# Two transformer-like layers on one core: who makes the sign tiles of the attention, where a head's sum stands, and where held sums and activation tables are prepared

## The reference, cut to what matters

```python
q, k, v = heads(x @ Wq + bq), heads(x @ Wk + bk), heads(x @ Wv + bv)      # 16 heads of 16
proj = gelu(x4.reshape(B, T, H * D) @ W1 + b1) @ W2 + b2                  # one score a token and head, of q and of k
q_proj, k_proj = (each centred, over one common deviation)
Z = concatenate([k_proj, q_proj]); idx = argsort(Z)
vc = v - mean(v over tokens)
# sorted by Z, with running sums: for each query the sum over all keys with a smaller score
context = z_q * cumsum(vc) - cumsum(vc * z)
norm = 2 * (z_q * cumsum(1) - cumsum(z)) - (z_q * total_v - total_vz)
context = 2 * context / max(norm, 1e-4)
```

## Time and profile before

| | us |
|---|---|
| median of 3 runs (lowest to highest) | 1379.29 (1377.48 to 1381.62) |
| the profiled execution | 1386.35 |
| its span | 1385.0 |
| PE busy, share of the span | 1080.4, 78% |
| DVE busy | 960.1, 69% |
| ACT busy | 818.6, 59% |
| POOL busy | 354.9, 26% |

### The profile page before, as it was taken

The page is one execution under the profiler, slowest core; times in us unless marked ns, Lnnn a source line. Parts: engine busy times, 40 slices in busy tenths (PEclk is TensorE's granted clock), DMA queues, the critical chain, the costliest instruction groups (busy, mean ns, idle before and its releaser), DMA issues. The chain is left out here.

```text
span 1385.0 us, 30980 instructions
## 1 busy us (share of the span) xinstructions
PE 1080.4 (78%) x12566; PEld 932.0 (67%) x12566; DVE 960.1 (69%) x1709; ACT 818.6 (59%) x957; POOL 354.9 (26%) x381
## 2 busy tenths in 40 slices
PE   5365689798898899979998897665548948983797
PEld 3254686598888887658888886554348845652797
DVE  5111686889999995889999996255626647843465
ACT  7111454699999954489999996143413326660332
POOL 3745001100000000200004401571644421345344
PEclk9689699899999999979999999795669979966799
DMA  8953400311212100012123213554243450013343
GB/s 252 340 149 122 157 1 0 74 63 63 93 63 94 63 2 0 4 62 94 63 74 113 90 67 101 199 199 145 89 135 104 120 179 1 1 47 108 112 119 100
DMA packets 83824, 133.72 MB, mean 97 GB/s; under 512 B 14083, under 2 KB 70403, under 8 KB 79043
## 3 DMA queue, kind: packets, MB, share of 16 engines
q1 hardware_dynamic: 65440, 91.27, 20.9%
q0 software_dynamic: 12960, 35.60, 7.1%
q10 hardware_dynamic: 5286, 4.88, 1.1%
HBM read 84.18 MB, written 47.54 MB: 95 GB/s over the span
## 5 line engine op out<-in xcount | busy, mean ns | idle before, releaser
L1655 ACT ACTIVATE b_signs<-b_q_everywhere,normed 128x2048 bf16<-128x2048 f32 x224 | 429.9, 1993 | 13.4 <-PE banks L1537 13.0
L1537 PE MATMUL banks<-b_value_parts,b_signs 128*128 128x102 bf16 x8192 | 398.3, 209 | 46.1 <-DVE b_signs L1872 39.6
L1537 PEld LDWEIGHTS banks<-b_value_parts,b_signs 128*128 128x128 bf16 x8192 | 377.9, 98 | 64.4 <-DVE b_signs L1872 49.1
L1872 DVE TENSOR_SCALAR b_signs<-b_q_everywhere,normed 128x2048 bf16<-128x2048 f32 x288 | 352.7, 1279 | 4.7 <-PE banks L1537 4.6
L850 POOL DMA_INDIRECT moe_slots<-normed,slot_of_token x128 | 135.7, 1060 | 39.1 <-issue 35.2
L1924 POOL MEMSET b_value_parts<- 128x256 bf16 x2 | 2.6, 1310 | 404.6 <-PE banks L1385 404.6
L415 PE MATMUL banks<-identity 128*128 128x128 f32 x264 | 45.7, 351 | 53.7 <-issue 24.3
L379 DVE BATCH_NORM_STATS2 ln_stats<-residual 128x6 f32<-128x256 f32 x192 | 71.4, 417 | 17.1 <-SPq L2147 9.7
L415 PEld LDWEIGHTS banks<-identity 128*128 128x128 f32 x264 | 44.2, 264 | 54.5 <-issue 33.5
L406 ACT ACTIVATE normed<-residual,ln_shift,ln_rstd 128x256 f32<-128x256 f32 x128 | 67.9, 592 | 11.9 <-DVE ln_shift L401 11.8
L487 PE MATMUL banks<-identity,normed 128*128 128x128 f32 x256 | 51.8, 338 | 25.5 <-ACT normed L406 21.1
(11 more groups left out here) (292 smaller groups left out, 2299.3 us busy)
## 6 DMA issues: line engine op xcount, KB each, us to landing
b_q_everywhere<-q_rows SPq DMA_DIRECT2D x32, 1024.0 KB
normed<-expert_rows SPq DMA_DIRECT2D x6, 1024.0 KB, 10.0
d_rows<-moe_slots SPq DMA_DIRECT2D x39, 129.5 KB
f_rows<-moe_slots SPq DMA_DIRECT2D x39, 129.5 KB
moe_slots<-a_empty SPq DMA_DIRECT2D x8, 518.0 KB, 10.3
a_rows<-moe_slots SPq DMA_DIRECT2D x16, 259.0 KB
c_rows<-moe_slots SPq DMA_DIRECT2D x16, 259.0 KB
expert_rows<-a_empty SPq DMA_DIRECT2D x1, 4096.0 KB
```

Of the source, the lines that this page charges most:

```text
L1537: ins = nc.tensor.matmul(banks[qt // QPB][:, qt % QPB * VP:(qt % QPB + 1) * VP], t.SG[:, (hh * TB + kt) % RING, qt * P:(qt + 1) * P], t.VO ...
L1655: nc.scalar.activation(t.SG[:, g % RING, :], t.QB[:, hh % 2, :], ACT.Sigmoid, bias=t.NKT[:, kt, hh % H:hh % H + 1], scale=STEEP).then_inc( ...
L1872: nc.vector.tensor_scalar(t.SG[:, g % RING, :], t.QB[:, hh % 2, :], t.KTM[:, kt, hh % H:hh % H + 1], 1.0, ALU.is_gt, ALU.mult).then_inc(s. ...
```

## The change

The diff, shortened where a line is only the new spelling of a count:

```diff
-WARM_SENT, WARM_ROWS, WARM_HEADS, WARM_PAIR = 16, 12, 28, 4
+WARM_SENT, WARM_ROWS, WARM_HEADS, WARM_PAIR, WARM_PARTS = 28, 16, 28, 4, 8
...
-DVE_KT = tuple(t for t in range(TB) if t not in ACT_KT)
+EVEN_HEADS = (6, 12, H - 1)
...
+def act_tiles(h):
+    return ACT_KT + (TB - 1,) if h in EVEN_HEADS else ACT_KT
+
+def dve_tiles(h):
+    return tuple(t for t in range(TB) if t not in act_tiles(h))
...
@@ pe_parts
             nc.tensor.matmul(value_bank(k, n - 1)[:, :], k.MINUSI[:, :], value_columns(t, n - 1, False, 1), start=False,
                              stop=True).then_inc(s.a_left, 1)
+        if n == 2:
+            pe_held(k, batch)
+        if n in (4, 6, 8):
+            if n == 4:
+                nc.tensor.wait_ge(s.held, batch + 1)
+            pe_warm(k, k.bank[4], WARM_PARTS)
@@ pe_held
-    nc.tensor.wait_ge(s.nkt, batch + 1)
     nc.tensor.wait_ge(s.qtm, batch + 1)
+    nc.tensor.wait_ge(s.ones_set, batch + 1)
+    nc.tensor.wait_ge(s.kz_third, batch + 1)
@@ pe_head
-        nc.tensor.wait_ge(s.ones_set, batch + 1)
-        nc.tensor.wait_ge(s.kz_third, batch + 1)
-        pe_held(k, batch)
     if hh >= 2:
         nc.tensor.wait_ge(s.sum, hh - 1)
-    if h == 1:
-        nc.tensor.wait_ge(s.held, batch + 1)
...
@@ act_attention
-            for kt in ACT_KT:
+            for kt in act_tiles(h):
                 act_sign(k, batch * H + h, kt)
@@ act_prepare
     if batch:
         act_norms_early(k)
+    nc.scalar.activation(t.ZS[:, 1:2], k.EPS[0:H, 0:1], ACT.Gelu)
     for n in range(steps + 1):
...
     for p in range(2, 4):
         act_part(k, batch, p, 0)
+    nc.scalar.activation(t.ZS[:, 1:2], k.EPS[0:H, 0:1], ACT.Sigmoid)
     for n in range(PAIRS + 1):
@@ dve_attention
-            for kt in DVE_KT:
+            for kt in dve_tiles(h):
                 dve_sign(k, hh, kt)
-                if h == 0 and kt == 6:
-                    dve_held(k, batch)
-                if h and kt == 2:
+                if h and kt == 4:
                     dve_sum(k, hh - 1)
                 for group in made:
-                    if kt in CONTEXT_KT:
+                    if kt in CONTEXT_KT and (h, kt) != (H - 1, CONTEXT_KT[-1]):
                         dve_context(k, batch, group, CONTEXT_KT.index(kt))
...
+        dve_context(k, batch, len(TOGETHER) - 2, len(CONTEXT_KT) - 1)
         dve_sum(k, batch * H + H - 1)
@@ dve_prepare, the loop over pairs
             dve_rest_of_values(k, batch, n + 1)
+        if n == 4:
+            dve_held(k, batch)
         if n == 2:
```

More of the change, by code:

```diff
@@ L132, in group_of, with act_made, dve_made @@
     return next(i for i, (lo, hi) in enumerate(TOGETHER) if lo <= h < hi)
+def act_tiles(h):
+    return ACT_KT + (TB - 1,) if h in EVEN_HEADS else ACT_KT
+def dve_tiles(h):
+    return tuple(t for t in range(TB) if t not in act_tiles(h))
+def act_made(hh):
+    return sum(len(act_tiles(i % H)) for i in range(hh))
+def dve_made(hh):
+    return TB * hh - act_made(hh)
 def cut_of(t):
@@ L1293, in sp_attention @@
             if h >= 2:
-                nc.sync.wait_ge(s.sign_d, len(DVE_KT) * (hh - 1))
-                nc.sync.wait_ge(s.sign_a, len(ACT_KT) * (hh - 1))
+                nc.sync.wait_ge(s.sign_d, dve_made(hh - 1))
+                nc.sync.wait_ge(s.sign_a, act_made(hh - 1))
             nc.sync.dma_start(t.QB[:, hh % 2, :], k.zq_rows[hh, :].partition_broadcast(P)).then_inc((s.qb_in0, s.qb_in1)[hh % 2], 16)
@@ L1531, in pe_head @@
                                  t.HELD3[:, h, :].unsqueeze(1).broadcast_to([P, QPB, 6]), start=False, stop=False)
-        if kt in ACT_KT:
-            nc.tensor.wait_ge(s.sign_a, len(ACT_KT) * hh + ACT_KT.index(kt) + 1)
+        if kt in act_tiles(h):
+            nc.tensor.wait_ge(s.sign_a, act_made(hh) + act_tiles(h).index(kt) + 1)
         else:
-            nc.tensor.wait_ge(s.sign_d, len(DVE_KT) * hh + DVE_KT.index(kt) + 1)
+            nc.tensor.wait_ge(s.sign_d, dve_made(hh) + dve_tiles(h).index(kt) + 1)
         for qt in range(TB):
@@ L1729, in dve_prepare @@
             if i == 0 and batch:
-                nc.vector.wait_ge(s.sign_a, len(ACT_KT) * H * batch)
+                nc.vector.wait_ge(s.sign_a, act_made(H * batch))
             z = t.Z[:, q, ch * BANK:(ch + 1) * BANK]
@@ L1865, in dve_sign @@
     g = hh * TB + kt
-    if kt == DVE_KT[0]:
+    if kt == 0:
         nc.vector.wait_ge((s.qb_in0, s.qb_in1)[hh % 2], 16 * (hh // 2 + 1))
```

## The result

The changed kernel takes 1373.32 us (median of 6 runs, 1368.7 to 1374.93); six runs of the kernel before, beside it, have a median of 1379.99. The ratio is 0.9957, with a 95% interval of 0.9942 to 0.9972: 0.43% faster, some 5.9 us by the ratio, where 9.8 were forecast. The profiled execution took 1373.54 (span 1372.3, mean granted clock 0.914). It is 12.8 us under that of before, more than the medians differ, because the stages outside the attention also came out shorter in it. These repeat within 0.1 to 0.4 us in the kernels that have the same code there, on three chips.

What follows compares the result with a forecast made beforehand. DVE was taken to bound the heads, ACT 3% behind, with ACT the bound in heads 0 to 2. Heads -8.5, start -2.7, GELU +1.45 gave -9.8 us: 1369.5, its own range 1366 to 1373, overall 1363.5 to 1376.5.

Steps and rivals of the forecast that it cites:

- The heads: Attention heads: moved sum and handed-over signs gain 2.2 us (batch 0), 3.9 (batch 1), 1.2 per last head; 8.5 in all.
- Rival A: Heads 3 to 14: ACT takes over as the bound, leaving a gain of 5.0 us, 1374.3; chance 0.22.
- The groups of head 6 and 12 keep 41.7: Sign that ACT bounds: three-head groups with a handed-over sign still take 41.7 us.
- The start of the heads: Each batch's first heads: early table load and moved held sums bring ACT's first sign 1.35 us earlier, 2.7 in all.
- take half of 2.95 at full clock: Value parts: PE's 16 held matmuls, moved there, take half of 2.95 us and end at 263.8.
- Rival D: Value parts: the clock falls despite the unread matmuls, 2.2 us less gain, 1371.7; chance 0.60 shared with the main forecast.
- The GELU: First rows of each batch: the unread GELU and its table load cost 1.45 us in batch 0, nothing in batch 1.
- The drain: ACT's table switches: the skill page adds a 1.38 us drain to each; by it the kernel would be 1.4 us faster.
- The runs of unread matmuls: Ahead of the expert stages: the longer warm-up runs lie hidden in PE's waits and change nothing, 0 us.
- rival B: Four expert stages: longer warm-up runs keep the clock up for the first rows, 6 us in all, 1363.5; chance 0.12.
- the sign set for B: Sign that the longer runs help: the stages before 190 and behind 845 change their length.
- Rival C: Heads: PE runs dry behind the third sign and its clock falls, +10.7 us each; one per batch 1390.9; chance 0.04.

Runs made afterwards that it cites:

- e3: The kernel before with only the edits of the head loops: 1372.76 us, ratio 0.9952.
- e5: The changed kernel with no signs handed over to ACT, the sum still behind the third sign: 1352.01 us, ratio 0.9972 to before on its chip.
- e6: The changed kernel with the sum behind the second sign again, signs still handed over: 1354.47 us, ratio 0.9984 to before on its chip.
- e12: e8 with one more sign handed to ACT, in head 9 of batch 1: 1364.32 us, ratio 0.9878 to the kernel before.
- e9: The changed kernel with the 16 held matmuls reading a contiguous block of ones, held values left wrong: 1367.82 us, ratio 0.9919 to before.
- e2: The changed kernel with the held values' matmuls and small steps back at head 0: 1369.01 us, ratio 0.9915 to the kernel before.
- e11: e8 with the 16 held matmuls shared between two accumulator banks, half of each held sum left out: 1365.37 us, a single run.
- e8: The changed kernel without the unread GELU and with the held values back at head 0: 1343.83 us, ratio 0.9903 to before on its chip.
- e1: The changed kernel without the unread GELU: 1370.49 us, ratio 0.9925 to the kernel before.
- e7: The changed kernel with the warm-up runs ahead of the expert stages short again (16 and 12 matmuls): 1349.54 us, ratio 0.9942 to before on its chip.
- e4: The changed kernel without the head-loop edits, except the moved last context step of group 4: 1379.41 us, ratio 1.0002 to the kernel before.

## Why the prediction was right, and where it was wrong

**The heads: right.** Forecast 2.2, 3.9 and 2 x 1.2, together 8.5; measured 1.97, 4.13, and 1.68 and 0.70 for the two last heads: 8.5. e3 shows the same 8.5 with nothing else changed. The reason held too: DVE bounds, the sum behind the third sign finds PE's tile done (0.1 of idle in e5), and the lost signs then count (e6 shows that they don't without it). Between DVE's sums a group of three heads takes 41.67 to 41.70 before; in the change it takes 40.60 where a sign is handed over and 41.79 where none is. The difference is the one sign of 1.20; the 0.12 more in every group comes with the sum's new place (e5 has 41.79 to 41.80 in all four), and it is why 1.97 came and not 2.4.

That the two last heads came to the forecast 2.4 is in part luck. Between DVE's sums head 15 takes 13.21 instead of 15.30 in both batches, 2.09 less. PE's start of head 15 cuts this into 1.68 and 0.70, as PE is 0.60 ahead of DVE's sum there in batch 0 and 1.59 ahead in batch 1 (0.20 in both before).

One reading was wrong. The prediction took ACT's 165.5 in batch 1 for a sum of overlapping durations, about 161 with two more signs. It is the time in which ACT was busy, the window less its idle time, and with the two signs it became 167.86 of 169.71: ACT was nearly as close to the bound as DVE. It did not spoil the 3.9.

**Rival A, ACT as the bound: false as to the sum, and the sign set for it was badly chosen.** "The groups of head 6 and 12 keep 41.7" came true between PE's starts: the group with head 6 takes 15.30 + 13.08 + 13.25 = 41.63, and a group without a handed-over sign 15.18 + 12.58 + 12.97 = 40.73. Between DVE's sums it is the other way round. The first group of batch 0, without a handed-over sign, and the second, with one:

```profile
319.57:361.36 41.79, 37.78 (x808) 36.35 (x806) 41.72 (x37) 41.17 (x23) 0.00 (x0) 1.00 0.22 86
361.36:401.96 40.60, 36.03 (x761) 34.15 (x759) 40.53 (x36) 40.60 (x22) 0.00 (x0) 1.00 0.19 73
```

In the second ACT is never idle, so A's mechanism is there. But PE enters this group 1.65 ahead of DVE's sum, where it entered the first 0.58 ahead, and this lead of 1.07 carries ACT's extra sign, as the prediction's argument against A had it. e12 leaves ACT almost no idle time in batch 1 and still brings what one sign is worth.

**The start of the heads: the step that failed.** It said that ACT's first sign gains 1.35 a batch, 2.7 in all; it lost 0.27 in batch 0 and gained 0.11 in batch 1. The failed term is "take half of 2.95 at full clock". I took the row's 2.95 for a matmul at half clock, as the clock stood at 0.53 there. It is 2.95 / 16 = 0.18 us each at either level, since the operand is read at every 17th element: 0.84 / 16 = 0.05 where it is contiguous (e9), 0.18 wherever it is not (e2, e11). The score stage ends 0.94 earlier in this trace, so on the clock of the earlier trace rows PE starts them at 261.14 + 0.94 = 262.1, where 262.3 was forecast, but DVE's first held step comes at 264.13 + 0.94 = 265.1 instead of 263.8. These 1.3 us are the 1.5 of the term less 0.2, DVE stands 1.97 for them, and they reach the first sign whole: in batch 1 it is (32.50 - 1.35) against 32.39, 1.24 late. The Trainium skill (Advanced Engine Details and Errata, SBUF Cachelines) says that accesses which each fall on another 16-byte line are penalised. Elements 34 bytes apart do so, and e9 fits it; the section gives no figure.

The rest of the step stands. Without the table load and with the clock up, the first sign comes 1.78 earlier (30.71), 1.4 of it from the load and 0.4 from the clock; I gave 1.8 as the end at which nothing of the held steps is exposed, and e9 is that case. The 0.4 is not in the prediction's working, which let the table load follow DVE's last third part. What ended last was ACT's own copy, and it had waited for PE at half clock:

```profile
275.55 0.60 ACT L1632 ACTIVATE b_value_parts<-banks 128x512 bf16<-128x512 f32 x1 [0.68 <-PE banks L1479]
```

(before; the load follows at 276.17). Of the two causes that I weighed, DVE's own steps cost nothing, and PE's matmuls, which I thought hidden, cost everything. Rival D, the clock falling all the same, was partly true in batch 0: 2.08 for the last pair's products, and the first sign 0.4 later than in batch 1. In e2, e8 and e9 these products take 1.12 or 1.13, behind 0.86 to 1.64 of idle instead of 2.27. With the held values in the value parts the idle time is 2.26 or 2.27 every time, and the products take anything from 1.12 (e1, first sign at 32.40) to 2.08. So, with the unread matmuls in place, a fall at these products was seen only with the stall for the held values, but it does not follow from the stall in every execution.

**The GELU: right in batch 0.** Forecast 1.45, measured 1.38 (37.50 - 36.12). In batch 1 its load stands in ACT's idle time, as forecast:

```profile
518.26 1.28 ACT L1610 ACT_TABLE_LOAD   x1
519.55 0.20 ACT L1610 ACTIVATE b_z_scale<-eps 16x1 f32<-16x1 f32 x1
527.85 1.08 ACT L1617 ACTIVATE b_q_or_k_T<-banks 128x512 fp32r<-128x512 f32 x2 [8.10 <-PE banks L1404]
```

But the rows stretch of batch 1 took 46.27 there and 46.39 in e7, against 44.84 before and 44.84 to 44.88 in e2, e4, e5, e6 and e9, which have the GELU as well. Windows from 5.85 us before the first rows to 7.15 behind them, of the changed kernel and of e2:

```profile
522.00:535.00 13.00, 10.91 (x52) 9.38 (x51) 7.74 (x11) 3.23 (x6) 0.00 (x0) 0.87 0.01 1
```

```profile
521.63:534.63 13.00, 10.90 (x60) 9.43 (x59) 8.14 (x12) 4.63 (x8) 0.00 (x0) 1.00 0.01 1
```

The clock fell for a moment in the one and not in the other, with the same code in this stage. Whether the change makes this likelier stays open: of the seven profiles with the unread GELU two have it (the change and e7), of the seven without it none, and no run was made to repeat one.

**No drain.** The drain that the prediction weighed beside its sum is not to be seen here: at 196.88 the load is followed by an activation 1.30 later and the next 0.11 behind that, and the load that left the path was worth 1.4, not 2.7.

**The runs of unread matmuls: right as to the time, and rival B is false as to its size.** e7 and the 1.97 at 878.62 show it. Two remarks: "2.5 to 5 us of idle stay" failed in the first block, where none stayed; and the sign set for B can't tell it from chance. The stages ahead of the attention and behind it are 2.3 and 4.9 us shorter in this profile, but e3, with the short runs, has 2.6 and 2.2 of this, and e7 lies among the kernels of its chip. **Rival C is false**: the clock is 1.00 in the windows of heads 3 to 15.

**The sum.** Inside the attention: heads -8.5, start +0.27 - 0.11, GELU +1.4, batch 1's rows +1.4, together -5.5. The ratio says -5.9 (3.9 to 8.0). With the start as forecast (-2.7) and without batch 1's rows it would be the -9.8.

## What to carry to other kernels

A duration read beside a low clock is not a clock-bound duration: before halving it, look for the same shape at full clock, or at what the instruction reads. Work moved to another place is costed by what waits for it there, on every engine that takes part. Two edits on a bound engine can be worth far more than the sum of each alone (batch 0: 2.76 against 0.20 + 0.24), or just the sum (batch 1): ask of each what wait appears once its work is gone. And measure a stretch at the engine that bounds it: another engine's starts move against it (here by up to 1.6 us), and gains seem to arise in heads where nothing was changed.

## What the runs showed that was not expected

- A matmul with a 96-column bf16 operand read at every 17th element takes 0.18 us, at full clock and at half, against 0.05 with a contiguous one (e9; e2, e11).
- A fall of the clock in the value parts costs 0.4 us a batch at the heads' start, though PE's products take twice as long: most of it lies in waits.
- One more sign moved in batch 1 (e12) seems to be worth 0.4 to 0.7 in heads 3 to 14 and another 0.8 in head 15 (14.77 to 14.01), six heads behind it, where nothing was edited. Between DVE's sums head 15 takes 13.2 in both kernels, and from the sum of head 2 to that of head 14 it is 169.31 against 170.50 to 170.74. So the gain is that of the one sign, 1.2 (1.4 against e8 itself), and lies in DVE's stream ahead of head 15, which PE starts 0.83 ahead of DVE's sum instead of 1.58.
